# Score products over all 128 rows, with one zero-padded block of keys per key head, in the two causal attention stages of a two-layer kernel

## What is computed

```python
# stage 0: 8 heads of 16, 4 key heads, window 128 with 4 sinks
k = jnp.repeat(k, N_REP, axis=1)
scores = jnp.einsum('bhtd,bhsd->bhts', q, k) * SCALE
scores = scores + head_scales[None, :, None, None] * (qp[..., :, None] * kp[..., None, :])
allowed = (j <= i) & ((j < SINKS) | (j >= i - WINDOW + 1))
attn = softmax(where(allowed, scores, -inf))
# stage 1: 16 heads of 8, 4 key heads, plain causal
k = jnp.repeat(k, rep, axis=2)
scores = jnp.einsum('bqhd,bkhd->bhqk', q, k) / np.sqrt(HD)
attn = softmax(where(tril, scores, min))
# stage 2: 16 heads of 8, 16 key heads, no mask
attn = softmax(einsum('bhsd,bhtd->bhst', q, k) / scale)
```

## Time and profile before

| | us |
|---|---|
| median of 3 runs | 2082.59 |
| lowest, highest | 2069.64, 2089.3 |
| the profiled execution | 2063.7 |
| its span, first to last instruction | 2061.9 |
| granted clock of PE over the span | 0.847 of 2.4 GHz |

### The profile page before, as it was taken

How to read it: one execution, slowest core, us unless ns; L and a number is a source line. 1 busy time by engine, 2 the same in 40 slices (tenths; PEclk the granted TensorE clock), 3 DMA queues, 4 the chain that set the end, 5 groups by cost and what they waited for, 6 DMA issues and landing times.

```text
span 2061.9 us, 32743 instructions
## 1 busy us (share of the span) xinstructions
PE 1778.0 (86%) x10932; PEld 1140.9 (55%) x10932; DVE 1016.9 (49%) x2471; ACT 724.5 (35%) x1533; POOL 391.8 (19%) x614
## 2 busy tenths in 40 slices
PE   5899999799999989989799999689898989997480
PEld 2555555445555545555588888555555555554260
DVE  2445454244444443444588888555545555553103
ACT  1243434314343443444322222234435343442130
POOL 2112121121211211211000000112122212113305
PEclk7799999759898986899899999768879787875695
DMA  7000000100000000000000000100000000100133
GB/s 223 28 5 3 4 3 6 31 6 3 7 4 7 4 8 1 1 1 1 1 1 1 0 0 1 57 0 5 9 6 9 5 10 5 29 1 20 64 101 82
DMA packets 37286, 38.65 MB, mean 19 GB/s; under 512 B 4561, under 2 KB 30449, under 8 KB 36753
## 3 DMA queue, kind: packets, MB, share of 16 engines
q1 hardware_dynamic: 35088, 32.54, 5.4%
q0 software_dynamic: 2048, 4.20, 0.7%
HBM read 28.27 MB, written 8.45 MB: 18 GB/s over the span
## 4 chain that ended last, share of the span: by engine, by line
PE 75%; DVE 9%; POOL 6%; issue 5%; ACT 2%; another core or an unknown queue 1%; DMA 1%; DVEq 0%; SPq 0%; POOLq 0%; ACTq 0%
PE ps_out L1845 12%; PE ps_max L1781 8%; PE ps_four L1008 6%; PE ps_max L1019 6%; PE ps_four L1734 5%; PE ps_four L1813 4%; PE ps_work L1690 4%; PE ps_four L1804 3%; PE ps_max L1771 3%; PE ps_work L1695 3%; PE ps_four L1715 3%; PE ps_work L1715 3%; DVE row_max L1587 3%; PE ps_max L1075 1%; PE ps_four L1066 1%
## 5 line engine op out<-in xcount | busy, mean ns | idle before, releaser
L1587 DVE TENSOR_REDUCE row_max<-ps_max 128x3 f32<-128x384 f32 (+1 forms) x640 | 375.0, 607 | 310.6 <-PE ps_max L1781 309.0
L1430 ACT ACTIVATE attn_f<-ps_four 128x384 f32<-128x384 f32 (+1 forms) x640 | 336.9, 532 | 456.3 <-PE ps_four L1813 452.9
L1845 PE MATMUL ps_out<-attn_f,v_all 128*9 128x256 f32 (+3 forms) x2560 | 331.3, 386 | 0.1
L1813 PE MATMUL ps_four<-q_st,k_st 26*128 26x256 f32 (+3 forms) x1280 | 324.4, 336 | 0.0
L1781 PE MATMUL ps_max<-k_st,q_st 24*128 24x256 f32 (+3 forms) x1280 | 285.9, 363 | 37.9 <-DVE row_max L1587 24.5
L1781 PEld LDWEIGHTS ps_max<-k_st,q_st 24*128 24x128 f32 (+1 forms) x1280 | 175.7, 213 | 205.4 <-issue 142.5
L1813 PEld LDWEIGHTS ps_four<-q_st,k_st 26*128 26x128 f32 (+1 forms) x1280 | 209.9, 203 | 34.5 <-issue 26.0
L1845 PEld LDWEIGHTS ps_out<-attn_f,v_all 128*9 128x9 f32 (+1 forms) x2560 | 103.4, 95 | 148.7 <-issue 51.8
L1771 PE MATMUL ps_max<-masks,ident_bf 128*128 128x384 bf16 x384 | 130.4, 369 | 36.5 <-DVE row_max L1587 31.4
L1019 PEld LDWEIGHTS ps_max<-wd,o_both 128*128 128x128 f32 x1024 | 134.7, 193 | 18.4 <-DVE o_both L910 7.9
L1019 PE MATMUL ps_max<-wd,o_both 128*128 128x128 f32 x1024 | 136.7, 277 | 5.8 <-DVE o_both L910 5.8
(11 more groups left out here) (235 smaller groups left out, 2518.9 us busy)
## 6 DMA issues: line engine op xcount, KB each, us to landing
wd<-in_L_ffn_W SPq DMA_DIRECT2D x16, 256.0 KB, 2.8
gates_all<-in_select SPq DMA_DIRECT2D x3, 1024.0 KB, 6.9
mod<-mod_dram SPq DMA_DIRECT2D x16, 192.0 KB, 3.1
x_all<-in_L_attn_x SPq DMA_DIRECT2D x8, 256.0 KB, 6.7
slots_dram<-attn_f SPq DMA_DIRECT2D x8, 256.0 KB, 5.4
mod<-mod_dram SPq DMA_DIRECT2D x16, 128.0 KB, 3.0
gates_all<-mod_dram SPq DMA_DIRECT2D x2, 1024.0 KB, 9.6
h_tok<-slots_dram SPq DMA_DIRECT2D x8, 256.0 KB, 3.0
```

The source lines that it names most:

```text
L1430: nc.scalar.activation(probs[:, h % 4, 0:w], ps_exp[:, h % 3, 0:w], ACT.Exp, scale=c.scale).then_inc(exp_done, 1)
L1587: nc.vector.tensor_reduce(row_max[:, r2, 0:blocks, h], src, AX_X, ALU.max).then_inc(max_done, 1)
L1813: ins = nc.tensor.matmul(bank[:, k * S:(k + 1) * S - first], k_st[rows, r, g, k * P:(k + 1) * P], q_st[rows, r, g, first:S], start=not c.c ...
L1845: last = nc.tensor.matmul(ps_out[base:base + c.hd + 1, at + first:at + S], v_tok[c.index][:, r, kb, h // (c.heads // c.kv), :], probs[:, h ...
```

## The change

In the causal stages (0 and 1) `k_st` now holds, for each of the 4 key heads, one group of 128 rows in which only that head's strip has data (keys in three slots, and the two rows of -1) and all others are zero. Query heads are placed so that heads that share a key head stand in the same strip of different groups (`place_of`). A score product can then run over all 128 rows: the foreign strips of `q_st` meet zeros. What else follows:

- The rows of -1 no longer come from ACT's bias but from the select products: POOL sets one row of `split` to 1.0 (`ones_row`, once for each causal stage, with its own waits and semaphore), and the key select products read 65 rows in stage 0 and 33 in stage 1, where they read 64 and 32.
- `max_place` has one table for each stage, 3 instead of 2 (loaded at the start and copied once by DVE).
- Stage 1 masks only blocks 0 and 2 of a bank, 256 columns instead of 384, and the zeroing of the masks' middle block and its wait are gone.
- A slot issues each maximum whole (mask and two products), and only then the exponential's wait, mask and products. `max_order` is the natural order.

The diff, cut to its core (`max_place_constant` gets the same placement, its tile 3 tables; `start` uses `masked_max`):

```diff
@@ -51,6 +51,20 @@
         self.pairs = heads // 2
         self.first = NB * index
 
+    def place_of(self, head):
+
+        rep = self.heads // self.kv
+        kv = head // rep
+        return kv // self.per_group * rep + head % rep, kv % self.per_group
+
+    def k_group(self, head):
+
+        return head // (self.heads // self.kv) if self.causal else self.place_of(head)[0]
+
+    def k_rows(self, base, extra):
+
+        return slice(0, P) if self.causal else slice(base, base + self.krows + extra)
+
     def q_cols(self):
         return 384 if self.causal else 512
 
...
@@ -92,26 +106,29 @@
 
     out = np.zeros((P, 3, 4, GROUPS, P), np.float32)
     for c in CFGS:
-        for g in range(GROUPS):
-            for j in range(c.per_group):
-                head = g * c.per_group + j
-                kv = head // (c.heads // c.kv)
-                for d in range(c.hd):
-                    for slot, (qp, kp) in enumerate(((0, 0), (0, 1), (1, 0))):
-                        row = j * c.strip + slot * c.hd + d
-                        out[head * c.hd + d, c.index, qp, g, row] = 1.0
-                        out[kv * c.hd + d, c.index, 2 + kp, g, row] = 1.0
+        for head in range(c.heads):
+            g, j = c.place_of(head)
+            kv = head // (c.heads // c.kv)
+            for d in range(c.hd):
+                for slot, (qp, kp) in enumerate(((0, 0), (0, 1), (1, 0))):
+                    row = j * c.strip + slot * c.hd + d
+                    out[head * c.hd + d, c.index, qp, g, row] = 1.0
+                    out[kv * c.hd + d, c.index, 2 + kp, c.k_group(head), row] = 1.0
+            if c.causal:
+                at = j * c.strip + c.krows
+                out[c.kv * c.hd, c.index, 2, c.k_group(head), at:at + 2] = -1.0
...
@@ -459,6 +476,8 @@
 
         def max_order(c):
 
+            if c.causal:
+                return list(range(c.heads))
             early, left, found = 3 * c.heads // 4, list(range(c.heads)), []
             for h in range(early):
                 taken = {h % c.per_group}
...
@@ -1198,6 +1217,14 @@
 
             pool.wait_ge(rotated, 1)
 
+            def ones_row(c):
+                if c.index > 0:
+                    pool.wait_ge(sel_mm, 4 * c.first)
+                    pool.wait_ge(ones_ready, c.index + 3)
+                m = c.kv * c.hd
+                nc.gpsimd.memset(split[m:m + 1, 1].bitcast(F32), 1.0).then_inc(minus_ready, 1)
+                pool.wait_ge(minus_ready, c.index + 1)
+
             def prep(c, b, r, name):
                 n, r2 = n_of(c, b), r % 2
                 if name == "stat":
...
@@ -1354,7 +1383,7 @@
                         at_least(act, values_mm, heads_until(c, b - RING))
                     dst = (q_st, k_st)[j // 2][:, r, 2 * (j % 2):2 * (j % 2) + 2, :]
                     src = work[bank_of(c, name)].rearrange("p (g s) -> p g s", g=2)
-                    if j < 2:
+                    if j < 2 or c.causal:
                         nc.scalar.copy(dst, src).then_inc(sel_out, 1)
                     else:
 
...
@@ -1624,9 +1653,6 @@
                 last.then_inc(mod_rows_dve, 1)
 
             def start(c):
-                if c.index == 1:
-
-                    nc.vector.memset(masks[:, :, 1, :], 0.0).then_inc(window_open, 1)
                 for name in prep_names(c):
                     prep(c, 0, 0, name)
                 for name, heads in opening(c):
...
@@ -1707,7 +1733,7 @@
                     last.then_inc(v_mm, 1)
                 if name[:3] == "sel":
                     j = int(name[3])
-                    i, rows = j // 2, (P, m)[j // 2]
+                    i, rows = j // 2, (P, m + 1 if c.causal else m)[j // 2]
                     if j % 2 == 0:
                         pe.wait_ge((q_lo, k_lo)[i], n + 1)
                     for g in range(2):
...
@@ -1766,20 +1792,21 @@
                     pe.wait_ge(sel_out, 4 * n_of(c, b) + 4)
                 at_least(pe, max_done, HEADS_BEFORE[c.index] + b * c.heads + i - 1)
 
-            def max_masks(c, i):
-                if c.causal:
-                    nc.tensor.matmul(ps_max[:, i % 2, 0:3 * P], ident_bf[:], masks[:, 0].rearrange("p n m -> p (n m)"),
-                                     start=True, stop=False, skip_group_check=True)
+            def put_masks(c, bank, side):
+
+                blocks = slice(0, 3) if c.window else slice(0, 3, 2)
+                nc.tensor.matmul(bank[:, 0:3 * P].rearrange("p (n m) -> p n m", n=3)[:, blocks, :], ident_bf[:],
+                                 masks[:, side, blocks, :], start=True, stop=False, skip_group_check=True)
 
             def max_scores(c, r, i, h, k):
 
-                g, base = h // c.per_group, (h % c.per_group) * c.strip
-                rows = slice(base, base + c.krows)
+                g, strip = c.place_of(h)
+                rows = c.k_rows(strip * c.strip, 0)
                 bank = ps_max[:, i % 2, :]
                 keys = slice(0, P) if c.causal and k == 0 else slice(0, S)
                 at = (0, P)[k] if c.causal else k * S
                 ins = nc.tensor.matmul(bank[:, at:at + keys.stop], q_st[rows, r, g, k * P:(k + 1) * P],
-                                       k_st[rows, r, g, keys], start=not c.causal, stop=True,
+                                       k_st[rows, r, c.k_group(h), keys], start=not c.causal, stop=True,
                                        skip_group_check=True)
                 if k == BLK - 1:
                     ins.then_inc(max_mm, 1)
...
@@ -1798,19 +1825,13 @@
                 else:
                     at_least(pe, exp_done, hn + 1 - (h + c.heads - max(k for k in range(c.heads) if k % 3 == h)))
 
-            def exp_masks(c, h):
-                bank = ps_exp[:, h % 3, :]
-                if c.causal:
-                    nc.tensor.matmul(bank[:, 0:3 * P], ident_bf[:], masks[:, 1].rearrange("p n m -> p (n m)"),
-                                     start=True, stop=False, skip_group_check=True)
-
             def exp_scores(c, r, h, k):
 
-                g, base = h // c.per_group, (h % c.per_group) * c.strip
-                rows = slice(base, base + c.krows + 2)
+                g, strip = c.place_of(h)
+                rows = c.k_rows(strip * c.strip, 2)
                 bank = ps_exp[:, h % 3, :]
                 first = P if c.causal and k == 1 else 0
-                ins = nc.tensor.matmul(bank[:, k * S:(k + 1) * S - first], k_st[rows, r, g, k * P:(k + 1) * P],
+                ins = nc.tensor.matmul(bank[:, k * S:(k + 1) * S - first], k_st[rows, r, c.k_group(h), k * P:(k + 1) * P],
                                        q_st[rows, r, g, first:S], start=not c.causal and k == 0,
                                        stop=True, skip_group_check=True)
                 if k == BLK - 1:
...
@@ -1820,15 +1841,27 @@
 
                 for i, _ in max_heads:
                     max_free(c, b + 1, i)
-                    max_masks(c, i)
                 exp_free(c, b, h)
-                exp_masks(c, h)
                 for k in range(BLK):
                     for i, head in max_heads[0:1]:
                         max_scores(c, (r + 1) % RING, i, head, k)
                     exp_scores(c, r, h, k)
                     for i, head in max_heads[1:]:
                         max_scores(c, (r + 1) % RING, i, head, k)
+
+            def masked_max(c, b, r, i, h):
+
+                max_free(c, b, i)
+                put_masks(c, ps_max[:, i % 2, :], 0)
+                for k in range(BLK):
+                    max_scores(c, r, i, h, k)
+
+            def masked_exp(c, b, r, h):
+
+                exp_free(c, b, h)
+                put_masks(c, ps_exp[:, h % 3, :], 1)
+                for k in range(BLK):
+                    exp_scores(c, r, h, k)
 
             def pair_values(c, b, r, p):
 
...
@@ -1931,7 +1966,12 @@
                 steps = tracked({bank_of(c, "place0"): (place_done, 2 * n + 1),
                                  bank_of(c, "place1"): (place_done, 2 * n + 2)})
                 for h, (max_heads, before, behind) in enumerate(slots(c, *flags(b))):
-                    scores(c, b, r, h, max_heads)
+                    if c.causal:
+                        for i, k in max_heads:
+                            masked_max(c, b + 1, (r + 1) % RING, i, k)
+                        masked_exp(c, b, r, h)
+                    else:
+                        scores(c, b, r, h, max_heads)
                     walk(c, b, r, *steps, before)
                     if h == 1 and flags(b)[0]:
                         pair_values(c, b - 1, (r - 1) % RING, c.pairs - 1)
```

29 lines of the change are left out of this document (17 added, 12 removed).

## The result

| | before | after |
|---|---|---|
| median, us (lowest to highest, 4 runs each) | 2082.11 (2069.64 to 2089.3) | 1928.24 (1924.26 to 1939.12) |
| profiled execution, us | 2063.7 | 1928.09 |
| its span, us, and granted clock | 2061.9, 0.847 | 1926.3, 0.871 |

The ratio is 0.9275 [0.9217, 0.9334]: faster. In the sessions of the experiments the kernel before had medians of 2067.84, 2068.39 and 2074.82 us, and a second series of the changed kernel (`after_again`) gave 1932.22 us, ratio 0.9345 [0.9282, 0.9408]. So some 10 to 18 of the first 154 us belong to the day, and the change is worth about 136 to 145.

What follows compares the result with a forecast made beforehand. PE was taken to bound the kernel, busy 1778.0 of 2061.9 us. Stage 1 blocks -45, stage 0 blocks -27, openings -10, clock -28 and fixed +2 gave -108, so 2082.6 - 108 = 1975 us; forecast 1940 to 2010, range 1925 to 2045.

Steps and rivals of the forecast that it cites:

- Rival A: Granted clock follows the rows in use, so it never falls in stage 1: -56 for -28, 1947 us; chance 0.12.
- Slots: Causal slots: one maximum from 0.85 to 0.70 us (stage 1) or 0.82 (stage 0); none, from 0.62 to 0.35 or 0.41.
- the terms -27 and -45: Blocks of the causal stages: 15 x -1.8 = -27 us in stage 0, 15 x -3.0 = -45 us in stage 1.
- The boundary: Block's start, slot 0: maxima's products ahead of the wait for placed maxima, -0.8 us a block in stage 0, -1.0 in stage 1.
- The clock: Stage 1: shorter boundary waits and gapless slots bring 2.4 GHz back sooner, half of 56 us, -28; bounds +20 and -56.
- The sum of -108: All terms on the profiled execution: -45, -27, -10, -28 and +2 us, giving 1956 us there.
- -10 and +2: Openings, where masks and maxima's products stand alone at 1.2 GHz: -10 us; fixed costs of loading and setup: +2 us.
- The fixed cost: Start and stage setup: larger `max_place` load 1 us, POOL's `ones_row` at most 0.5 us a stage; +2 us.
- The 19 us between profile and median: Profiled execution lay 19 us under the median; unable to split it, the forecast subtracted 108 from the median 2082.6.
- (B): Rival on stage 1's clock: it doesn't profit, +20 for -28, 2023 us; chance 0.10.
- (C): Rival: other engines set the pace; half of the 72 us in blocks lost, clock gives nothing, 2039 us; chance 0.10.
- (D): Rival: weights can't load beside the product before, each 256-column product costs 0.22 us; slower, 2115 us; chance 0.05.

Runs made afterwards that it cites:

- wait_first: Changed kernel, with slot 0's wait for the placed maxima and the exponential's bank moved back ahead of the maxima's products: 1956.24 us, ratio 0.9441.
- old_order: Changed kernel with the former order in a slot (masks ahead, products by turns), still full height and narrow masks: 1944.16 us, ratio 0.9403.
- rows_only: Changed kernel with the former slot order and stage 1 masks of 384 columns, so placement, padding and full height alone: 1965.86 us, ratio 0.948.
- rows65: Changed kernel with stage 1's score products over 65 rows instead of 128, heads 8 to 15 using scores of heads 0 to 7: 1962.64 us, ratio 0.9492.
- strip_rows: Changed kernel with only the row range undone, each score product of stages 0 and 1 reading its head's own strip: 2395.96 us, ratio 1.1595.
- before_mask256: Kernel before the change, with stage 1's masks narrowed to 256 columns: 2155.18 us, ratio 1.0372.
- masks384: Changed kernel with stage 1's masks back at 384 columns, the middle block zeroed by DVE: 1931.66 us, ratio 0.934.

## Why the prediction was right, and where it was short

Forecast 1975 us, measured 1928 (ratio 0.9275 for a forecast 0.948): the sign and the range held, at its lower end, 3 us above its bound of 1925. Rival A's 1947 us lay nearer. The terms of the slots and of stage 0 came as worked out; the clock's size is in part luck, since its cause was another.

*Slots: right.* Expected in stage 1 0.35, 0.70 and 1.10 us, found 0.30, 0.66 without the gap to the values products, and 1.16 in the block's first slot; in stage 0 0.82 with one maximum, found 0.74. The choice between 0.12 and 0.22 for a product behind a mask was on the high side even at its lower end: 0.04 us.

*Blocks: right.* 18.5 and 29.0 us at 2.4 GHz for 18.9 and 28.9; the terms -27 and -45 came out as -29.6 and -45.

*The boundary: right in stage 0, half right in stage 1.* The wait of 0.85 us went, and wait_first prices it at 0.8 to 0.9 a block for -0.8. In stage 1 DVE's wait shrank from 1.08 to 0.51 us, as reckoned (-0.6), but little of it reached the end: there wait_first prices the wait at 0.2 us a block and old_order the whole order at 0.6, for -1.0. PE's waits for a bank in a warm block of stage 1, before and after (us in total, times, longest):

```profile
PE ps_max L1771 <- DVE row_max L1587: 1.7, 2, 1.0
```

```profile
PE ps_max L1798 <- DVE row_max L1616: 1.1, 1, 1.1
```

The long wait stayed, a shorter one went. PE's idle time fell from 31.9 - 29.27 = 2.6 to 29.1 - 26.90 = 2.2 us, its busy time by 2.4. So the block came out right from two terms that were off: -0.4 where -1.0 was reckoned for the boundary, and -2.4 where -2.0 was for the work.

*The clock: the right size, from a cause not weighed enough.* -28 was taken as half of 56, found -34. The prediction named shorter waits and gapless slots as the cause and gave rival A, the rows, 0.12. The shorter waits did not do it: with the old boundary order the clock of stage 1 is at its best (0.97 in old_order and rows_only). Gapless slots are not enough: rows65 keeps every gap closed and falls back to 0.88, so rows count by themselves. How much of the step from strips to 65 rows, 647 us at 1.2 GHz in strip_rows to 114 in rows65, belongs to the rows and how much to the closed gaps, no run separates. The streamed columns of the masks count too: over strips 397 us for 148 (before_mask256), over full height in the new order 45 to 54 for 27 (masks384). Rival A's sum, no fall at all, did not come true either: 54 us at 1.2 GHz remain.

*The terms that were missing.* The sum of -108 was 27.6 us short of the span's -135.6. Of these 6 are the clock and 3 stage 0; the rest lies outside the 15 block periods, where only -10 and +2 stood. The last block of each stage has only slots without maxima, 8 x 0.21 and 16 x (0.62 - 0.35) = 1.7 and 4.3 us by the prediction's own prices, and was left out of "15 x"; the stretch that holds the second, from the end of the 15 periods to the first placing of maxima in stage 2, 387.2 us long before, is 381.6 now. The opening of stage 0 and the way between the stages (-7.0 and -11.6 instead of some -1 and -7) are in good part at 1.2 GHz, the latter at a granted clock of 0.63 before and 0.73 now; how much of the two is the clock was not worked out. In stage 1's opening two maxima stand 371.98 - 371.35 = 0.63 us apart (before 1.16; expected 0.70). What remains, and the 2.4 us behind 381.6, was not taken apart.

*The fixed cost: right.* PE's first matmul waits 14.69 us for the load, 0.8 more than in the earlier trace rows, for 1 us.

*The 19 us between profile and median* were left in the forecast as they were. The changed kernel's profiled time is its median, and the kernel before came to 2068 in two later sessions and 2075 in a third: most of that gap was the spread of its first session, and a forecast from the profiled time alone would have been 1956.

*Rivals.* (B) asked for +20 and (C) for half the blocks' gain: neither shows, PE's share stays 86%. (D), that weights can't load beside the product before, had 0.49 us for a mask and its two products in stage 1; they take 0.35 for a maximum and 0.30 for an exponential.

*The rule on weight loads.* The Trainium skill ("TensorE: Matmul & The Clock Gate", Part 3, The mechanism) says that a weight load overlaps matmuls in flight only when the row groups differ; the same section also lets a load go ahead of them into a background weight buffer. By the first sentence rival D would have come true, 2115 us, and the measurement decides against it. The prediction read 0.22 us between two products of one strip as agreement with it. That reading was wrong: the first two of four select products over 128 rows stand 0.22 us apart as well, and in one strip of 64 rows four products, each with a load of its own, take the same 0.73 us as over 128. In one of 32 rows, in the second stage of the kernel before, they take no longer:

```profile
611.50 0.53 PEld L1715 LDWEIGHTS ps_four<-split,select 32*128 32x128 f32 x4
611.56 0.68 PE L1715 MATMUL ps_four<-split,select 32*128 32x256 f32 x4
```

So what slows strip_rows against the changed kernel at 2.4 GHz is, as far as these rows show, the number of changes of height, and not loads that wait within a strip.

## What to carry to other kernels

Where products over few rows stand between matmuls over all rows, price the changes of height (here a gap of 0.09 us each, and some 0.1 us more in the pair behind one) before praising their concurrency: zero-padding to full height took them away and cost next to nothing. Judge a change of TensorE's work at both clock levels, since fewer rows or fewer streamed columns, even with the same or less time in every warm block, can cost more in granted clock than they save. Price the parts of a change together, and don't forget openings and last blocks outside "N times a block".

## What was not expected of the hardware

- The granted clock depends on how many rows the products use, with the same instructions, and the same timing and busy time in a warm block: 65, 97 and 128 rows gave 0.88, 0.89 and 0.94 in stage 1 and medians of 1963, 1945 and 1930 us.
- PE's modelled busy time says little about it: 787 of 789 us busy went with 0.59 and 852 of 854.5 with 0.57, while 427 of 457 went with 0.97. Nor can one fall be argued from what stands just before it. Windows: of rows65, ending at a fall; then of the changed kernel, ending at a fall, at the same place of the next block where 2.4 GHz held, and ending at a fall at the loop's branch:

```profile
426.50:429.50 3.00, 1.71 (x15) 0.94 (x14) 2.21 (x6) 1.22 (x6) 1.09 (x3) 1.00 0.03 9
```

```profile
453.00:456.00 3.00, 1.57 (x14) 0.94 (x14) 1.87 (x5) 1.45 (x6) 1.62 (x3) 0.99 0.10 28
486.80:489.80 3.00, 1.58 (x14) 0.94 (x14) 1.87 (x5) 1.45 (x6) 1.62 (x3) 1.00 0.11 33
664.60:667.60 3.00, 0.38 (x8) 0.16 (x3) 0.20 (x1) 0.00 (x0) 0.00 (x0) 1.00 0.02 5
```

  The same work (1.57 and 1.58 us busy) was followed once by a fall and once not; only the sum over a stage is firm.
- A bf16 mask and the fp32r product behind it start 0.04 us apart when both use all rows, and 0.25 us apart when the product uses 48.
- Four products in one strip of 32 or 64 rows, each with its own weights, follow each other as fast as over 128 rows, 0.12 us apart after the first.
